# Fewer TensorE signals in the tile loops of two expert layers, with one layer's TensorE order rearranged

## What is computed

```python
# layer 1: 8 experts, 2 per token, I = 512; ternary weights, activations rounded to 8 bits
def expert_ffn(x, gw, uw, dw):
    gate = bitlinear(x, gw)
    up = bitlinear(x, uw)
    activated = up * jnp.square(jax.nn.relu(gate))
    return bitlinear(activated, dw)          # rounds `activated` by its row's largest value first

# layer 2: 7 experts, 3 per token, H = 256, and a shared expert of the same form
def _expert_ffn(x, w1, wg, w2):
    return jax.nn.silu(x @ w1) * (x @ wg) @ w2
```

## Time and profile before

| | |
|---|---|
| median of 3 runs | 1120.05 us (1119.65 to 1120.12) |
| the profiled execution | 1128.99 us |
| its span, first to last instruction | 1127.2 us |
| mean granted TensorE clock | 0.921 |
| layer 1's tile loop, about | 433 to 558 us |
| layer 2's tile loop, about | 824 to 997 us |

### The profile page before, as it was taken

One profiled execution on the slowest core, in us unless ns is written; L12 is line 12 of the kernel. 1 busy time (PEld: TensorE's weight loads), 2 busy tenths in 40 slices (PEclk: granted clock), 3 DMA queues, 4 the chain that ended last, 5 costly groups with the idle time before them and its releaser, 6 DMA issues. The chain is left out here.

```text
span 1127.2 us, 20348 instructions
## 1 busy us (share of the span) xinstructions
PE 906.5 (80%) x5845; PEld 685.0 (61%) x5861; DVE 776.8 (69%) x2020; ACT 603.6 (54%) x1385; POOL 445.3 (40%) x518
## 2 busy tenths in 40 slices
PE   5767989968999675766788899978998897996187
PEld 4556779967777443544465566646876776763165
DVE  6756648867887688767678886666844354339987
ACT  4663347755444386777835566665234543423385
POOL 3166624440000105666446526511066666534400
PEclk9988989988999898899979999999999998985599
DMA  9954557766200031222290001021052522251001
GB/s 283 157 168 135 160 170 215 220 205 199 71 20 1 1 85 34 62 60 61 79 291 11 10 26 50 1 66 38 1 178 85 154 89 77 76 193 64 0 20 57
DMA packets 95972, 109.19 MB, mean 97 GB/s; under 512 B 14270, under 2 KB 85843, under 8 KB 95875
## 3 DMA queue, kind: packets, MB, share of 16 engines
q1 hardware_dynamic: 84162, 76.76, 23.4%
q0 software_dynamic: 11712, 31.20, 8.8%
HBM read 73.89 MB, written 34.03 MB: 96 GB/s over the span
## 5 line engine op out<-in xcount | busy, mean ns | idle before, releaser
L3257 DVE TENSOR_TENSOR f_act<-f_silu,bank 128x256 f32<-128x256 f32 x54 | 22.7, 421 | 84.1 <-ACT f_silu L3174 58.7
L3125 POOL DMA_INDIRECT f_got<-f_tokens,f_places x54 | 53.9, 998 | 60.4 <-DVE f_places L946 44.3
L3131 POOL DMA_INDIRECT f_outputs<-f_y,f_places x54 | 56.5, 1047 | 53.2 <-ACT f_y L3188 36.9
L1284 POOL DMA_INDIRECT f_outputs<-f_y,f_places x39 | 41.3, 1060 | 58.1 <-ACT f_y L1334 36.1
L2087 POOL DMA_INDIRECT f_got<-f_tokens,f_places x39 | 42.3, 1085 | 51.0 <-DVE f_places L946 37.8
L2522 POOL TENSOR_TENSOR work<-work 128x512 f32<-128x512 f32 x32 | 33.0, 1063 | 71.0 <-ACT work L2572 71.0
L3174 ACT ACTIVATE f_silu<-bank 128x256 f32<-128x256 f32 x54 | 20.9, 387 | 63.3 <-PE bank L3347 42.0
L2328 PE MATMUL bank<-tern,f_xq 128*128 x146 | 42.3, 412 | 15.2 <-ACT f_xq L2125 6.1
L2095 POOL DMA_INDIRECT f_outputs<-f_y,f_places x39 | 39.3, 1007 | 36.2 <-ACT f_y L2150 26.4
L2670 DVE TENSOR_REDUCE work<-bank 128x8 f32<-128x512 f32 x64 | 43.4, 679 | 12.8 <-PE bank L2768 12.6
L3347 PE MATMUL bank<-f_rhi,f_xT_hi 128*128 x108 | 45.0, 417 | 2.4 <-DVE f_xT_lo L3198 2.2
(11 more groups left out here) (557 smaller groups left out, 3174.7 us busy)
## 6 DMA issues: line engine op xcount, KB each, us to landing
f_back<-f_outputs SPq DMA_DIRECT2D x21, 256.0 KB, 4.8
f_back<-f_outputs SPq DMA_DIRECT2D x10, 512.0 KB, 6.5
f_got<-f_sorted SPq DMA_DIRECT2D x39, 129.0 KB
f_sorted<-clear_row SPq DMA_DIRECT2D x1, 4992.0 KB, 26.2
raw<-in_L_ffn_w SPq DMA_DIRECT2D x24, 176.0 KB
tern_raw<-in_L_ffn_gate_w SPq DMA_DIRECT2D x8, 512.0 KB
tern_raw<-in_L_ffn_up_w SPq DMA_DIRECT2D x8, 512.0 KB
tern_raw<-in_L_ffn_down_w SPq DMA_DIRECT2D x8, 512.0 KB
```

The costliest lines, as they stand in the source:

```text
L1284: pool.indirect_dma_start(g.outputs, bass.IndirectOffsetOnAxis(ap=dest[:, j:j + 1], axis=0), y_out[:, j % OUT_RING, :], None).then_inc(gon ...
L3125: pool.indirect_dma_start(got[:, j % GATHERS, :], None, tokens, bass.IndirectOffsetOnAxis(ap=sorter.token[:, j:j + 1], axis=0)).then_inc(s ...
L3131: pool.indirect_dma_start(outputs, bass.IndirectOffsetOnAxis(ap=sorter.dest[:, j:j + 1], axis=0), y_out[:, j % OUT_RING, :], None).then_in ...
```

## The change

Layer 1: the signal behind the gate's matmuls is gone; `scalar_relu` waits for the one behind the up product. The signals behind the turn and the second product are gone too. What was told by them is told by the signal of the rows in, which moves to the step's end and is called `stepped`; only the last seven tiles' second products add to it as well, since no rows come in any more. TensorE's order in a step becomes up, turn, second product, rows in; ScalarE's `scalar_back` moves ahead of `scalar_in`. Layer 2: TensorE's order stays. The turn is told by the next rows in, the second product of tile i by the first product of tile i+3; ScalarE copies y_out(j-3) right behind silu(j), where it copied y_out(j-2) at the step's end. Layer 3 only has a count changed that began where layer 1's semaphore stood.

```diff
+            TURN_LAG, DOWN_LAG, IN_LEAD = 4, 5, 2
+            def step_at(j):
+                return j + IN_LEAD + 1
+            def turned_at(i):
+                return step_at(i + TURN_LAG)
+            def down_at(i):
+                return step_at(i + DOWN_LAG)
...
             def scalar_relu(act, j):
-                act.wait_ge(s.gate, ternary.PER * E + j + 1)
+                act.wait_ge(s.up, j + 1)
...
             def scalar_back(act, j):
-                act.wait_ge(s.turned, j + 1)
+                act.wait_ge(s.stepped, turned_at(j))
                 if j >= 2:
-                    act.wait_ge(s.down, j - 1)
+                    act.wait_ge(s.stepped, down_at(j - 2))
...
             def scalar_out(act, j):
-                act.wait_ge(s.down, j + 1)
+                act.wait_ge(s.stepped, down_at(j))
...
             def tensor_up(pe, j, at):
-                for m, b, signal in ((GATE, 1, s.gate), (UP, 3, s.up)):
+                for m, b in ((GATE, 1), (UP, 3)):
...
-                    mm.then_inc(signal, 1)
+                mm.then_inc(s.up, 1)
...
             def tensor_down(pe, j, at):
-                mm.then_inc(s.down, 1)
+                if j + DOWN_LAG + IN_LEAD >= NT:
+                    mm.then_inc(s.stepped, 1)
...
             # layer 2
+            def turned_at(i):
+                return i + 4
+            def down_at(i):
+                return i + 4
...
-                for j in range(NT + 2):
+                for j in range(NT + 3):
...
+                    if j >= 3:
+                        i = j - 3
+                        act.wait_ge(s.up, down_at(i))
+                        if i >= OUT_RING:
+                            act.wait_ge(gone[i % FLIGHT], gone_up_to(i - OUT_RING))
+                        act.activation(y_out[:, i % OUT_RING, :], bank[6 + i % 2][:, 0:D], ACT.Copy).then_inc(s.out, 1)
                     if 1 <= j <= NT:
                         i = j - 1
-                        act.wait_ge(s.turn_ps, i + 1)
+                        act.wait_ge(s.in_ps, turned_at(i))
...
-                        tp.then_inc(s.turn_ps, 1)
+                        if j + 2 >= NT:
+                            tp.then_inc(s.in_ps, 1)
...
-                        mm.then_inc(s.down, 1)
+                        if j + 1 >= NT:
+                            mm.then_inc(s.up, 1)
```

More of the change, by code:

```diff
@@ L2009, in layer1_experts @@
                 p.kept0, p.kept1, p.shift, p.rounded, p.rowed, p.mask, p.ranks, p.chain, p.which, p.hot, p.inverse, p.slots,
-                s.in_ps, s.xq, s.out, s.acc0, s.back0, s.back1, s.back2, s.back3, s.stat
+                s.stepped, s.xq, s.out, s.acc0, s.back0, s.back1, s.back2, s.back3, s.stat
             ) = early.of("kept0 kept1 shift rounded rowed mask ranks chain which hot inverse slots "
-                         "in_ps xq out acc0 back0 back1 back2 back3 stat")
+                         "stepped xq out acc0 back0 back1 back2 back3 stat")
             p.kept = (p.kept0, p.kept1)
             (
-                s.raw, s.size, s.total, s.chain, s.gate, s.tern, s.shifted, s.w_tp, s.w, s.up, s.relu, s.once,
-                s.prod, s.peak, s.pair, s.rate, s.turned, s.wholeT, s.down, s.acc1
+                s.raw, s.size, s.total, s.chain, _, s.tern, s.shifted, s.w_tp, s.w, s.up, s.relu, s.once,
+                s.prod, s.peak, s.pair, s.rate, _, s.wholeT, _, s.acc1
             ) = whole_sems
@@ L2060, in layer1_experts @@
             after.w_tp = after.w = 3 * E
-            after.up = after.relu = after.peak = after.wholeT = after.down = after.shifted = after.turned = NT
+            after.up = after.relu = after.peak = after.wholeT = after.shifted = NT
+            after.down = after.turned = 0
             after.pair = after.rate = PAIRS
@@ L2121, in scalar_in @@
             def scalar_in(act, j):
[L2122 removed]
+                act.wait_ge(s.stepped, j + 1)
                 if j >= 2:
@@ L2335, in tensor_turn @@
                 for c in range(IC):
-                    tp = pe.transpose(bank[5 + j % 2][:, c * P:(c + 1) * P], shifted[:, j % 2, c * P:(c + 1) * P], ident[:, :])
-                tp.then_inc(s.turned, 1)
+                    pe.transpose(bank[5 + j % 2][:, c * P:(c + 1) * P], shifted[:, j % 2, c * P:(c + 1) * P], ident[:, :])
             def tensor_down(pe, j, at):
@@ L2376, in tensor @@
                     tensor_in(pe, j)
-                for j in range(NT + 5):
+                for j in range(NT + DOWN_LAG):
                     if j < NT:
                         tensor_up(pe, j, where[j])
[L2380 to L2385, removed]
+                    if 0 <= j - TURN_LAG < NT:
+                        tensor_turn(pe, j - TURN_LAG)
+                    if 0 <= j - DOWN_LAG:
+                        tensor_down(pe, j - DOWN_LAG, where[j - DOWN_LAG])
+                    if j + IN_LEAD < NT:
+                        tensor_in(pe, j + IN_LEAD)
                     if j + 1 < NT:
@@ L3182, in scalar @@
                         scalar_in(act, j + 2)
[L3183 to L3188, removed]
                     if j in SIZES_AT:
@@ L3701, in vector_shift @@
                 dve.wait_ge(s.rate, was.rate + T + 1)
-                hold(dve, s.turned, was.turned + T - 1)
+                if T >= 2:
+                    hold(dve, s.turned, was.turned + T - 1)
                 dve.tensor_scalar(shifted[:, k % 2, :], hidden[:, k % 2, :], rate[:, j], MAGIC, ALU.mult, ALU.add).then_inc(s.shifted, 1)
```

16 lines of the change are left out of this document (8 added, 8 removed).

## The result

The changed kernel takes 1132.67 us (median of 4 executions, 1130.12 to 1135.37), the kernel before 1120.09 us beside it (4 executions): ratio 1.0113, 95% interval 1.0089 to 1.0137. It is slower by 12.6 us, where 1101 was forecast.

A forecast was written before the change was run, and what follows sets the result against it. Late TensorE signals, about 1.45 us each, were taken to stall layer 1's and 2's loops. -19 - 6 + 2 = -23 us on the profiled 1128.99, scaled by 0.83 to -19, gave 1101 us; range 1081 to 1123.

The forecast's parts named there:

- The excess: Time of late-signal steps over undisturbed ones: 31.5 us in layer 2's loop, 20 us in layer 1's.
- the price per signal: Both loops: each late TensorE signal takes about 1.45 us, so four cost 5.8 us a step, two 2.9.
- -19 us: Layer 2's loop: fewer signals shorten a slow step from 4.83 to 3.35 us, leaving 12.7 of 31.5 us.
- The assumed share of 0.3: Share of steps taken to be slow after the change in both loops; before it 0.26 in layer 2, 0.21 in layer 1.
- the first rival: GpSimd's DMAs, not the number of signals, make signals late; nothing is saved, about 1122 us; chance 0.12.
- less than 25 us: Sign in layer 2's loop: ScalarE's silu waits, 42.0 us in all before, fall below 25 us with a shorter longest wait.
- The granted clock: Sign in both loops: it rises from 0.93 and 0.94 if TensorE pauses less.
- Layer 1's -6 us: Layer 1's loop: two signals instead of five make a slow step 3.75 us against 5.01, leaving 14 of 20 us.
- The relu's later signal: Layer 1: relu waits some 0.4 us longer, for the up product; covered in the loop, open once in the fill.
- The link that I feared: Layer 1's loop: one signal links steps, 2.3 + 1.45 us when late; as the slower rival up to 1160 us, chance 0.12.
- Fill and drain, +2 us: Layer 1's fill and drain: later waits cost 2 us, bounds 0 and 5, with a drain pitch of 1.85 us against 1.46.
- Layer 2's later waits: Layer 2's loop: `y_out` some 1.4 us later delays scatter and gather, with about half a step of cover; nothing booked.

The follow-up runs named there:

- e13: The kernel before, unchanged, run once more on chip 13: 1120.72 us, ratio 0.9996.
- e17: The kernel before with only layer 1's new order, all five signals kept, on chip 15: 1076.52 us, ratio 1.0011.
- e4: The kernel before with four more signals a tile in layer 2's loop, to a semaphore nobody waits for, chip 8: 1123.13 us, ratio 1.0016.
- e3: The kernel before with only the change's layer 2 edits, on chip 8: 1125.25 us, ratio 1.0031.
- e15: The kernel before with only the change's layer 2 edits, on chip 13: 1123.83 us, ratio 1.0029.
- e16: The kernel before with 46 of layer 2's row gathers and TensorE's waits for them left out, on chip 13: 1097.21 us, ratio 0.9777.
- e1: The kernel before, unchanged, run again on chip 8: 1125.34 us, ratio 1.0025.
- e11: The kernel before with only layer 1's new order, all five signals kept, on chip 2: 1077.71 us, ratio 1.0005.
- e2: The kernel before with only the change's layer 1 edits and layer 3's skipped wait, on chip 8: 1129.54 us, ratio 1.0080.
- e9: The whole change again, against the kernel before, on chip 2: 1085.28 us, ratio 1.0075.
- e14: The kernel before with the change's layer 1 part, but the gate's own signal kept for relu, on chip 13: 1126.48 us, ratio 1.0058.
- e10: The kernel before with layer 1 signalling twice a tile in the order of before, on chip 2: 1095.58 us, ratio 1.0169.

## Why the prediction was wrong

**The excess was read rightly.** Layer 2's and layer 1's loop were said to hold 31.5 and 20 us over an undisturbed 2.55 and 2.5 us a tile. Where no signal is late, kernels with these loops unchanged or in the new order run them in 134 to 137 and 91 to 91.5 us, 2.5 to 2.6 and 2.4 a tile. The two levels differ by little else: from the first load to the last result copy, the two loops take 124.2 + 161.5 us in e13 and 103.2 + 140.3 in e17 (layer 1 in the new order, which costs nothing there), 42.2 less, with 41.0 us between the spans of these two profiles (1115.1 and 1074.1).

**The step that failed is the price per signal.** "Each takes about 1.45 us" made four signals 5.8 us and two 2.9, a long step 3.35 instead of 4.83, -19 us. Doubling the signals (e4) changes nothing that the measurement tells, halving them (e3, e15) gains nothing, and removing GpSimd's gathers (e16) removes the stall, from 13 long steps to 1. The assumed share of 0.3 was right, 16 long steps of 53; but each kept its length: a long step of layer 2 takes 4.1 to 4.2 us on average with two signals (e3, e15) and 4.1 to 4.4 with four (e1, e13), where 3.35 was forecast. The profile after shows most late signals coming at once, when GpSimd has stopped (12 of 14, 0.60 to 1.35 us after its last DMA). This is the first rival, which had 0.12. For it stood and the earlier trace rows; I let one picture in the earlier trace rows, four copies 1.45 us apart, outweigh them, although one stretch can't tell "one delay each" from "one release each". Such evenly spaced copies come again in e1 and e13, and in neither kernel with two signals (e3, e15); the time is the same, and what spaces them stays open. The total of silu's waits, 42.0 us, was no sign of lateness either, only the longest was: without late signals the total is 44.7 (e11), so "less than 25 us" could hardly have come true. The granted clock rose to 0.94 and 0.98, as another sign had it, but TensorE is no busier for it (143.71 of 164 us in layer 2, 146.69 of 167 before), and e13 has 0.99 there with nothing changed.

**Layer 1's -6 us** fell by the same step, and in its place stands a loss that I had booked at nothing: its loop is 2.6 to 4.1 us longer in every profile that has its part of the change (after, e2, e9, e14), and where signals are late its drain 2 us. The relu's later signal was called covered; alone it adds 2 us to the loop where no signal is late, and the drain gives 1 to 2 of them back. What is left of the loss, by subtraction, comes from the later telling of turn and second product. The link that I feared, a step of 3.75 us on a late signal, is not what costs: the loss in the loop is about the same without late signals (e9).

**Fill and drain, +2 us,** was right for the drain: 2.3 us, at a pitch of 1.9 instead of 1.85. On chips 6, 2 and 15 the drain is as long with layer 1 as before (11.1 to 11.8), so there it is no loss.

**Layer 2's later waits** were booked at nothing with "half a step of cover". They may cost 0.3%: e3 and e15 read 1.0031 and 1.0029, each interval just off 1, but e3 is level with e1, which changes nothing.

**Without a price per signal,** 1120 us and my 2 us for the later waits make 1122, the first rival's time, which I held to be unlikely for the sake of the earlier trace rows. e4 agrees with the rival here (1.0016, an interval that holds 1): four more signals a tile cost nothing that shows. The result is 10.7 us over 1122, and the parts put most of that on layer 1's later waits, to which I gave 2 us.

**What stays open.** The order alone and the gate's signal alone have run only where no signal is late, e14 only where they are, so layer 1's loop is not split in the same way on both sorts of chip. What makes signals late on one chip and not on another, with GpSimd's DMAs at least as dense, is not known. Nor is all of the loss placed: loop and drain of layer 1 hold 5.4 of e2's 9 us. No kernel tried here is faster than before by more than the measurement tells, apart from those that leave gathers out.

## What to carry to other kernels

Taking signals away was no gain here; the consumer then waits for a later instruction, and where that closes a ring (e10, 3.06 us a tile instead of 2.4) it is a loss. Before halving anything for a price per piece, double it once: an experiment of a few lines would have shown that the number has no price here (e4, 1.0016). And this stall of TensorE and ScalarE gave way to an edit of GpSimd, the engine that issues DMAs without a rest (e16, loop 2 from 156.5 to 134.6 us), not to edits of what waits.

## What the runs showed of the hardware

Beside the result and on chips 8 and 13, TensorE's signals were seen late while GpSimd issued indirect DMAs one behind the other, up to 12 in a row in loop 2 (a silu 3.14 us after its product; 9 to 16 long steps in loop 1). With two signals a tile most of the silus that began over 0.5 us after their product with ScalarE idle began 0.6 to 1.4 us after its last DMA: 12 of 14 beside the result, 11 of 18 in e3 and in e15. On chips 6, 2 and 15 no kernel had a long step in loop 1, although GpSimd issued up to 65 DMAs in a row in loop 2 there (e11). The kernel before took 1120 to 1122 us on the ones and 1075 to 1078 on the others. The ratios of this kernel must therefore be taken on one chip, and a change that works on the stall had nothing to work on at the others.
